# Six graph layers on one core: weights prepared beside the first graphs, all four streams started at once, and an order of its own for the beginning and the end

## What is computed

```
layer 0  (GAT)         h = norm(x); q,k,v = h Wq, h Wk, h Wv; 12 heads; softmax(q k + beta*adj, masked by adj) v;  x += result
layers 1, 2 (DIR)      left = h Wl, right = h Wr; u = triu(h.left) + tril(h.right); a = exp(u)*adj / sum; c = a (h Wlin); norm(c)
layers 3, 4 (DIG)      u = h.h; a = softmax(u)*adj / sum; c = upper(a)(h Wl) + diag(a)(h Ws) + lower(a)(h Wr); norm(c)
                       x += relu(norm(...)) after layers 2 and 4
layer 5  (GRAPHORMER)  12-head attention with adj added to the scores, masked; x + attention Wo + bo is the output
```

## Time and profile before

| | us |
|---|---|
| median of three runs (3014.38 to 3015.76) | 3015.51 |
| the profiled execution's own time | 3016.85 |
| its span, first to last instruction | 3015.1 |

### The profile page before, as it was taken

The page is one execution under the profiler, slowest core; times in us unless marked ns, Lnnn a source line. Parts: engine busy times, 40 slices in busy tenths (PEclk is TensorE's granted clock), DMA queues, the critical chain, the costliest instruction groups (busy, mean ns, idle before and its releaser), DMA issues.

```text
span 3015.1 us, 88804 instructions
## 1 busy us (share of the span) xinstructions
PE 2874.9 (95%) x34304; PEld 2231.5 (74%) x34304; DVE 2493.4 (83%) x6895; ACT 1769.2 (59%) x6484; POOL 1397.1 (46%) x2313
## 2 busy tenths in 40 slices
PE   0699999999999999999999999999999999999996
PEld 0577777777777777777777777777777777777774
DVE  7478888888888888888888888888888888888874
ACT  3355665566566566566556656656656655665653
POOL 0145445444444544544544445454454454444443
PEclk9799999999999999999999999999999999999997
DMA  6000000000000000000000000000000000000000
GB/s 212 1 2 14 14 8 14 14 8 14 14 12 11 14 12 10 14 14 8 14 14 8 14 14 12 11 14 12 11 14 14 8 14 14 8 14 14 12 7 9
DMA packets 36091, 50.00 MB, mean 17 GB/s; under 512 B 3680, under 2 KB 35552, under 8 KB 35552
## 3 DMA queue, kind: packets, MB, share of 16 engines
q1 hardware_dynamic: 26464, 31.73, 3.4%
q10 hardware_dynamic: 9216, 12.59, 1.1%
HBM read 31.72 MB, written 12.58 MB: 15 GB/s over the span
## 4 chain that ended last, share of the span: by engine, by line
PE 92%; DVE 4%; POOL 1%; DMA 1%; ACT 1%; issue 1%; SPq 0%; POOLq 0%; DVEq 0%
PE bank L827 65%; PE bank L938 8%; PE bank L884 6%; PE bank L851 4%; PE bank L900 3%; PE bank L876 3%; PE bank L929 1%; PE bank L906 1%; PE bank L889 1%; DVE w_lo L647 1%; ACT t L563 1%; DMA t<-in_weights_dram 0%; DMA beta_col<-in_beta_dram 0%; DVE t L639 0%; DVE means L635 0%
## 5 line engine op out<-in xcount | busy, mean ns | idle before, releaser
L827 PE MATMUL bank<-w_hi,ht 128*128 128x384 f16 x3840 | 1032.9, 327 | 1.3 <-DVE t L707 1.3
L827 PE MATMUL bank<-ht,w_hi 128*128 128x128 f16 x9216 | 836.9, 220 | 12.1 <-DVE ht L685 8.2
L827 PE MATMUL bank<-ht,w_lo 128*128 128x128 f16 x4608 | 806.6, 220 | 0.0
L827 PEld LDWEIGHTS bank<-ht,w_hi 128*128 128x128 f16 x9216 | 721.0, 98 | 62.3 <-issue 29.2
L827 PE MATMUL bank<-w_lo,ht 128*128 128x384 f16 x1920 | 627.5, 327 | 0.0
L563 ACT ACTIVATE t<-t,few 128x128 f32<-128x128 f32 x1536 | 596.0, 398 | 0.7 <-DVE few L716 0.6
L827 PEld LDWEIGHTS bank<-w_hi,ht 128*128 128x128 f16 x3840 | 376.6, 98 | 231.3 <-issue 2.6
L449 POOL TENSOR_TENSOR v<-v,row 128x384 f32<-128x384 f32 x256 | 256.8, 1003 | 572.2 <-ACT v L530 572.2
L827 PEld LDWEIGHTS bank<-ht,w_lo 128*128 128x128 f16 x4608 | 454.0, 99 | 0.0
L554 ACT ACTIVATE qk<-bank 128x256 f16<-128x256 f32 x576 | 218.2, 379 | 301.4 <-PE bank L827 301.4
L544 ACT ACTIVATE ht<-bank 128x384 f16<-128x384 f32 x384 | 188.2, 490 | 320.4 <-PE bank L851 318.9
(11 more groups left out here) (108 smaller groups left out, 5384.1 us busy)
## 6 DMA issues: line engine op xcount, KB each, us to landing
x<-in_x_dram SPq DMA_DIRECT2D x64, 192.0 KB, 2.3
out_dram<-h ACTq DMA_DIRECT2D x64, 192.0 KB, 1.9
t<-in_weights_dram SPq DMA_DIRECT2D x19, 576.0 KB, 4.9
adj<-in_adj_dram SPq DMA_DIRECT2D x64, 64.0 KB, 2.2
row<-in_rows_dram SPq DMA_DIRECT2D x1, 3648.0 KB, 11.5
bias_qk<-in_qk_bias_dram SPq DMA_DIRECT2D x1, 3.0 KB, 11.2
beta_col<-in_beta_dram SPq DMA_DIRECT2D x1, 0.5 KB, 11.0
```

Of the source, the lines that this page charges most:

```text
L827: m = nc.tensor.matmul(out, a, b, start=(first and n == 0), stop=(last and n == 3 * len(left) - 1))
```

## The change

1. Setup is written as pieces (`set_up` of SP, DVE and ACT) that the order tables call for with the mark `w`, in between steps of graphs. Nobody waits for the whole setup; in its first graph each step waits for the matrix (`wait_weights`) and the row (`wait_row`) that it reads. The row that layer 0 needs is loaded first, by itself.
2. The staging places are no longer in the streams' tiles: they are the parts of `w_hi` and `w_lo` that belong to matrices 15 to 18, and one new tile `spare`. The means are subtracted on ACT (three activations of 128x384 for a matrix, eight for the rows) and no longer on DVE.
3. The order tables are `OPENING`, `BODY` repeated 14 times, and `CLOSING`. `BODY` is the old `TURNS`, and at its first step the streams stand where `LATE` had them (54, 42, 30 and 18 PE steps done). `OPENING` has the same 144 PE steps as the old beginning in an order of its own. `CLOSING` has the last full round and the 72 steps after it, 288 in all, in an order of its own.
4. To make room, `PT` (the transposed probabilities) now lies in `T`, and `PARTS`, `RT` and `OH` in `QK`; `B0` has a tile of its own. One wait of ACT's flip on POOL's sums goes. Several semaphores are merged (`turn_hi`, `proj_hi` and `mixed_hi` into `high`, and so on); each still counts instructions of one engine.

```diff
-TURNS = {
-    "tensor": ("201231121320210030123032032203030101101321322010003003312302232031321101230103103310101212212032"
+OPENING = {
+    "tensor":
+        "100000100001000110110000101210320132212033012020111001103021122321311102100100020321212302030020"
+    "vector":
+        "wwwww1001www01www0wwww0www0w0wwww0010w0w010w0w011w01101102020302323302111021230321w2100211200110"
...
+    "sync":
+        "wwwww10wwwwwwwwwwwwwwww",
 }
...
+REPEATS = 14
...
+    for mark in OPENING[engine] + BODY[engine] * REPEATS + CLOSING[engine]:
+        if mark == "w":
+            yield None
+        else:
+            s = int(mark)
+            n, k = divmod(taken[s], len(own))
+            taken[s] += 1
+            yield s, n, own[k]
...
-        PT = [sb(f"pt{s}", [P, H, P]) for s in range(STREAMS)]
+        B0 = [sb(f"edge{s}", [P, G, P]) for s in range(STREAMS)]
...
+        PT = [t[:, 0] for t in T]
+        flat_qk = [q[:].rearrange("p w c a t -> p (w c a t)") for q in QK]
+        PARTS = [q.bitcast(F32).rearrange("p (h k) -> p h k", h=H) for q in flat_qk]
+        RT = [q[:, 2 * D:4 * D].bitcast(F32).rearrange("p (c k) -> p c k", c=C) for q in flat_qk]
...
+        places = [w_hi[:, 15:17], w_hi[:, 17:19], w_lo[:, 15:17], w_lo[:, 17:19]]
+        places = [x.rearrange("p w c n -> p (w c n)").bitcast(F32) for x in places] + [spare[:]]
+        def place_of(w):
+            return {15: 3, 16: 1, 17: 4, 18: 4}.get(w, w % 4)
+        def wait_weights(eng, r, w):
+            if r == 0:
+                eng.wait_ge(w_lo_done, w + 1)
+        def wait_row(eng, r, k):
+            if r == 0 and k == 0:
+                eng.wait_ge(first_in, 48)
+            elif r == 0 and k in range(1, 9):
+                eng.wait_ge(rows_centred, k)
+            elif r == 0:
+                eng.wait_ge(rows_in, 16)
...
+        def run(engine, step_of, pieces=iter(())):
+            for turn in turns_of(engine, plan.steps):
+                if turn is None:
+                    next(pieces)
+                else:
+                    s, r, step = turn
+                    step_of(r, s, *step)
...
+            def set_up():
+                sp.dma_start(bias_qk[:], qk_bias).then_inc(first_in, 16)
+                sp.dma_start(beta_col[:], beta.rearrange("(a b) -> a b", a=1).broadcast_to((P, 1))).then_inc(first_in, 16)
+                sp.dma_start(row[:, 0:1], rows_v[:, 0:1].broadcast_to((P, 1, D))).then_inc(first_in, 16)
+                yield
+                for w in range(N_W):
+                    earlier = place_users[place_of(w)]
+                    if earlier.index(w) > 0:
+                        sp.wait_ge(w_lo_done, earlier[earlier.index(w) - 1] + 1)
+                    if w == 15:
+                        sp.wait_ge(w_lo_done, 15)
+                    sp.dma_start(stage_of(w), w_v[w]).then_inc(w_in[place_of(w)], 16)
+                    yield
+                    if w == 2:
+                        sp.dma_start(row[:, 1:N_ROWS], rows_v[:, 1:N_ROWS].broadcast_to((P, N_ROWS - 1, D))).then_inc(rows_in, 16)
+                        yield
...
-            pool.wait_ge(setup_done, 1)
...
+                    if w in CENTRED_W:
+                        act.wait_ge(w_sums, 2 * CENTRED_W.index(w) + 2)
+                        for c in range(C):
+                            mean = means[:, 8 + CENTRED_W.index(w) * C + c:9 + CENTRED_W.index(w) * C + c]
+                            nc.scalar.activation(stage_of(w)[:, c], stage_of(w)[:, c], ACT.Identity,
+                                                 bias=mean).then_inc(w_centred, 1)
+                        act.wait_ge(w_centred, C * (CENTRED_W.index(w) + 1))
+                    nc.scalar.activation(w_hi[:, w], stage_of(w), ACT.Copy, scale=WS).then_inc(w_hi_done, 1)
...
-                    if layer == GRAPHORMER and c == 0:
-                        wait_for(act, r, s, "sums", ("scores", layer, g), C + 1)
...
-                nc.vector.tensor_tensor(stage[w % 4], stage[w % 4], mean.unsqueeze(2).broadcast_to((P, C, D)),
-                                        ALU.add).then_inc(w_centred, 1)
```

451 lines of the change are left out of this document (232 added, 219 removed).

## The result

| | us |
|---|---|
| before, median of 4 runs (3014.38 to 3015.92) | 3015.64 |
| changed, median of 4 runs (2960.24 to 2963.99) | 2963.26 |
| ratio, 95% interval | 0.9825 (0.9808 to 0.9842) |
| profiled execution of the changed kernel: own time, span | 2963.42, 2961.7 |

The time fell by 52.4 us, 1.7%; forecast were 2964.5 us, within 2936 to 2992. Two terms of the sum, though, were off by more than the total shows.

The account below looks back on a forecast made before the run. PE was taken to bound the rounds, leaving 343 us at both ends to win from. Gains of 48 us at the beginning, 0 in the rounds and 3 at the end gave 2964.5 us against a 3015.5 us median; range 2936 to 2992.

Parts of the forecast that it names:

- When the first graph can start: Start of the beginning: rows landed at 17.5 us, two graphs 1.4 us later, first matmul at 19 to 20 us.
- DVE's queue up to stream 0's scores: Beginning: DVE's queued setup and graph steps, 55 us with 2 us of wait, put stream 0's scores at 57 us.
- From scores to layer 1: Beginning: 15.1 us as for stream 0 alone, two or three `w_lo` fitting DVE's idle time; turn at 72 us.
- What is lost after it: Beginning after stream 0's turn of layer 1: 13 us lost beyond PE's 105 us, half of the old loss of 28.
- The sum's 48: Whole beginning: ends at 190 us instead of 238, so 48 us gained, between 32 and 61.
- The subtraction on ACT: Setup: moving the mean subtractions from DVE to ACT spares DVE 10.9 + 3.4 = 14.3 us.
- The rounds: The repeated rounds: order and bank sequence stay the same, costed at 0, at most 3 us won or lost.
- The end: Closing steps: 3 us gained, between 0 and 5, inside stream 3's layer 2; no order shortens its last layer.
- the account of banks: Rounds: 240 banks a round are whole turns through eight, so the same banks follow each other; costed at 0.
- (a): Rival, beginning: DVE alone sets it, ending between 157 and 177 us; time 2931 to 2951 us; chance 0.17.
- (b): Rival, beginning: setup holds graphs back, up to 22 us more, ending at 206 to 235; 2981 to 3010 us; chance 0.15.
- (c): Rival, rounds: new tile places lengthen each round; 3.6 us a round cancels the gain, worse case 3046 us; chance 0.03.

Follow-up runs that it names:

- e7: The changed kernel with the means of matrices and rows subtracted on DVE again instead of ACT: 2970.87 us.
- e2: The changed kernel with all setup ahead of the first graph step and the old order of the 144 beginning steps: 3012.55 us.
- e3: The changed kernel with all setup ahead of the first graph step, keeping the new order of the 144 beginning steps: 2991.94 us.
- e1: The changed kernel with the old order for the end alone, the last full round and the 72 steps after it: 2965.83 us.
- e9: e1 with the old bank rule (bank by place in the round) put back in the closing steps: 2969.14 us.
- e4: The changed kernel with the first two graphs loaded ahead of the 18 rows, and ACT's and DVE's row handling moved later: 2963.73 us.
- e5: The changed kernel with setup pieces pushed back towards the layer that needs them, and streams 2 and 3 loading before the last matrices: 2971.95 us.

## Why the prediction was right, and where it was not

**When the first graph can start: 1.2 to 1.8 us off.** Forecast were the rows at 17.5 us and the first matmul at 19 to 20; it was 19.29 for the rows' sums and 20.15 for the matmul. The same 5376 KB took 1.7 us longer than by the rows that the forecast used. The forecast let the graphs land 1.4 us behind the rows; they were there 0.9 us behind them, so the transfers seem to have shared the time. Whether that is the 1.7 us wasn't tried.

**DVE's queue up to stream 0's scores: the right engine, and a time that is partly luck.** Scores at 57 us, found 56.76; the next `w_lo` not before 26.5 with 2 us of wait, found at 28.12 with 2.47. But DVE began 1.8 us late, at the rows, and needed 33.9 us from the end of the rows' sums to the scores, where the forecast had 35.9. It was 2 us too dear because it misread a column: the 6.6 us given for stream 0's own steps are PEld's 6.63 in the earlier trace rows; DVE's there is 4.24. On DVE the steps of both streams took 6.5 us in that stretch, not 8.6. With both figures put right the same sum gives 56.6. e7 confirms the mechanism: 14.3 us more on DVE move the scores by 11.4 us and the start of the rounds by 9.8.

**From scores to layer 1: too short.** Forecast 15.1 us, as when stream 0 was alone; it took 18.6, so the turn stood at 75.4 us, not at 72. The step that failed is the sentence that the two or three `w_lo` there fit into DVE's idle time (there are four); and the pieces of setup on ACT were not asked about at all. DVE's timeline of the changed kernel, behind it POOL's, and ACT's of the changed kernel and of before at the first exponential:

```profile
70.32 0.56 DVE L821 TENSOR_TENSOR x<-t,x 128x384 f32<-128x384 f32 x1
70.80 1.35 DVE L711 SCALAR_TENSOR_TENSOR w_lo<-w_lo,w_hi 128x1152 f16<-128x1152 f32 x1
72.07 0.55 DVE L741 BATCH_NORM_STATS2 few<-x 128x6 f32<-128x384 f32 x1
...
72.94 1.35 DVE L711 SCALAR_TENSOR_TENSOR w_lo<-w_hi 128x1152 f16<-128x1152 f32 x1
74.73 0.48 DVE L750 TENSOR_SCALAR h<-x,few 128x384 f32<-128x384 f32 x1 [0.44 <-POOL few L526]
```

```profile
30.11 1.08 POOL L526 TENSOR_TENSOR few<-few,powers 128x1 f32<-128x1 f32 x2
...
73.10 1.59 POOL L526 TENSOR_TENSOR few<-few,powers 128x1 f32<-128x1 f32 x1 [16.29 <-DVE few L743]
```

```profile
60.00 1.16 ACT L591 ACTIVATE w_hi<-w_lo 128x1152 f16<-128x1152 f32 x1
61.07 0.39 ACT L644 ACTIVATE t<-t,few 128x128 f32<-128x128 f32 x1
```

```profile
88.97 0.40 ACT L563 ACTIVATE t<-t,few 128x128 f32<-128x128 f32 x1 [0.62 <-DVE few L716]
```

One `w_lo` stands between the new `x` and its statistics, 1.3 us. A second runs while POOL takes the root of the variance, on a tile of one column; POOL's instruction takes 1.59 us and not its usual 0.55, 1.04 more. Those are 2.3 of the 3.5 us. The rest comes before the new `x`: ACT's first exponential starts 4.3 us after DVE begins the scores (56.76 to 61.07), with two `w_hi` and a matrix's subtraction in front of it, though DVE's reduction that it needs ends at 59.4. Before, it started 2.7 us after (86.26 to 88.97), as soon as DVE was done. Of these 1.6 us 1.3 are left when DVE adds to `x`. The meeting with POOL is what the Trainium skill, "SBUF — State Buffer", section "Who interferes with whom", would have: the two exclude each other for the whole instruction. By that rule, the trace agrees: POOL's ended 0.40 us after DVE's. It does not agree everywhere: the second of POOL's two at 30.11 ran until 31.19, a `w_lo` began on DVE at 30.85, and both took their usual 0.55 and 1.35 us; there POOL had begun first. The forecast's estimate of three such meetings, 4 us, was too dear: only one on stream 0's way to its turn of layer 1 cost anything.

**What is lost after it: 10 us, not 13.** From 75.4 to 190.2 it took 114.8 us for the 105 of PE's own work. With the 3.4 us late before it, the sum came out at 190 for 190. So two misses of three us with opposite signs met there, as two of 2 us had met before the scores; the 13 was half of an old loss and not worked out from anything in the new order. The sum's 48 is right as a mechanism and owes its exactness to luck. e2 and e3 show what carried it: 18.6 of the us are the order and 30.5 the overlap; the forecast had them in one.

**The subtraction on ACT.** It was taken as DVE's relief of 14.3 us. That holds only beside graph steps (9.8 us, e7); with setup by itself, and all else of the new setup with it, nothing was won (e2, rounds 1.3 us later than before).

**The rounds: right**, at 0 within the 4 us that traces of the same rounds differ by.

**The end: a term of 3 us, bound 0 to 5, measured 7.7.** The order's part came out at 3.4 us, near the forecast, but not where the forecast had it: it took all of it from stream 3's layer 2 and held that no order shortens what follows. From e1 to the changed kernel layer 2 is 2.2 us shorter, layer 3 2.1 and layer 4 1.1, the last layer 0.4 longer, and 1.5 are lost ahead of layer 2. What failed outright is the account of banks. The prediction saw that 240 banks a round are thirty turns through eight, so that nothing changes in the rounds, and stopped there. It did not ask what the old rule, a bank by place in the round, had done where part of the round is missing. The bank waits were to be seen in before's end: a wait of a flip for an eviction that it does not read. That rule cost 4.3 us (e9).

**The rivals.** (a), DVE alone sets the beginning, would have ended it by 177: it did not, but e7 shows DVE's queue as what paces the first 60 us. (b), setup holds the graphs back, was there for 3.4 us of DVE's waits for `w_hi` between the first matmul and the scores (2.47 of them at one `w_lo`; 3.4 more came before any graph), and for the 1.6 us on ACT behind the scores, not for 22. In e4, where DVE's waits grew to 15.7 us, a first matmul 8 us earlier brought nothing. (c), longer rounds, did not come.

## What to carry to other kernels

When buffers are given out by a step's place in a repeated round, look at the first and last passes, where steps are missing: an instruction that waits for the reader of something it has nothing to do with is the sign, and dealing buffers in turn over the steps that really run removed it here. Work moved from a busy engine to an idle one shortened nothing here while both handed the same piece back and forth with nothing between; it paid once other work lay there. Hurrying one stream ahead, at the price of idle time on the engine that paces the stretch, lost more than it won (e5; the reason is argued only). A number that comes out right can be two misses: check each term of a sum against the trace, and each figure against its column. And an experiment for each end apart, with cuts at the same step of the order in every trace, tells some 1.5 us where the medians tell 3.

## What was not expected of the hardware

A POOL instruction on a tile of a single column took 1.59 us beside a DVE instruction of 128x1152 with both inputs in SBUF that had begun 0.16 us before it; its median is 0.55 us, and it took that too when it had begun before such a DVE instruction. Being small doesn't spare it; beginning first did. And fillers that raised the last layer's granted clock from 0.73 to 0.87 shortened that layer by 1.4 us only, and the closing steps by 0.3.
